# A fused attention and feed-forward layer on one core: the projection of batches 1 to 3 moved, in one-bank pieces, between the attention turns of the batch before

## What is computed

```
x = x + _layernorm(attention(_layernorm(x)))     # x: 4 batches, 1024 tokens, 256 channels, f32
  q, k, v = binlinear(x, W, b)                   # W replaced by mean|W| of its row times sign(W)
  16 heads of 16: softmax(q k^T * 0.25) v, then binlinear(y, Wp, bp)
x = x + _layernorm(ffn(_layernorm(x)))
  h = silu(tlin(x, w1)) * tlin(x, w2)            # 256 -> 1024, ternary weights, a scale for each row
  h = gelu(tlin(h, h1)); h = gelu(tlin(h, h2))   # 1024 -> 1024
  tlin(h, w3)                                    # 1024 -> 256
```

## Time and profile before

| | |
|---|---|
| median of 3 runs | 1319.59 us (1319.3 to 1322.22) |
| the profiled execution | 1320.33 us, its span 1318.6 us |
| PE busy | 1195.9 us (91%) |
| ACT busy | 770.9 us (58%) |
| DVE busy | 558.4 us (42%) |
| POOL busy | 35.0 us (3%) |

### The profile page before, as it was taken

The page is one execution under the profiler, slowest core; times in us unless marked ns, Lnnn a source line. Parts: engine busy times, 40 slices in busy tenths (PEclk is TensorE's granted clock), DMA queues, the critical chain, the costliest instruction groups (busy, mean ns, idle before and its releaser), DMA issues.

```text
span 1318.6 us, 19216 instructions
## 1 busy us (share of the span) xinstructions
PE 1195.9 (91%) x6696; PEld 734.9 (56%) x6696; DVE 558.4 (42%) x1013; ACT 770.9 (58%) x920; POOL 35.0 (3%) x30
## 2 busy tenths in 40 slices
PE   4965999999999999964999999989999999999997
PEld 3741222222222222212788888878888878888886
DVE  7941112111111112043664766727657457475633
ACT  4955999999999999964423324224342243332421
POOL 5220000000000000000000000000000000000000
PEclk9986999999999999977999999989999989999999
DMA  5998576667777776712000101001001001010000
GB/s 159 351 274 209 111 150 129 117 117 141 129 129 129 134 153 120 156 46 64 1 33 0 45 20 34 33 2 33 32 1 64 1 30 36 1 32 1 13 4 16
DMA packets 49946, 107.19 MB, mean 81 GB/s; under 512 B 5856, under 2 KB 22624, under 8 KB 49880
## 3 DMA queue, kind: packets, MB, share of 16 engines
q1 hardware_dynamic: 49880, 106.31, 34.8%
HBM read 71.91 MB, written 45.88 MB: 89 GB/s over the span
## 4 chain that ended last, share of the span: by engine, by line
PE 51%; DVE 1%; issue 1%; ACT 0%; DVEq 0%; ACTq 0%
PE ffn_ps L1136 23%; PE ffn_ps L1137 23%; PE ffn_ps L1164 2%; PE ffn_ps L1165 2%; PE side_ps L1120 1%; PE side_ps L1129 1%; DVE ln_stats L1273 0%; DVE zn L1284 0%; DVE zn L1325 0%; DVE x L1308 0%; DVE zn L1298 0%; DVE x_lo L1315 0%; DVE zn L1301 0%; DVE zn L1335 0%; DVE ln_mean_var L1277 0%
## 5 line engine op out<-in xcount | busy, mean ns | idle before, releaser
L912 ACT ACTIVATE probs<-s_ps 128x1024 f32<-128x1024 f32 x512 | 471.5, 1131 | 25.8 <-PE s_ps L863 25.7
L1137 PE MATMUL ffn_ps<-h_lo,W 128*128 128x512 f32 x1024 | 401.1, 392 | 0.0
L1136 PE MATMUL ffn_ps<-h_hi,W 128*128 128x512 f32 x1024 | 401.1, 392 | 0.0
L872 PE MATMUL y_ps<-probs,v_st 128*17 128x512 f32 x2048 | 273.1, 605 | 37.2 <-DVE y_sb L949 10.0
L1227 ACT ACTIVATE hid<-ffn_ps,scales 128x512 f32<-128x512 f32 x128 | 81.0, 685 | 232.6 <-PE ffn_ps L1137 227.7
L1136 PEld LDWEIGHTS ffn_ps<-h_hi,W 128*128 128x128 f32 x1024 | 192.4, 188 | 42.0
L1137 PEld LDWEIGHTS ffn_ps<-h_lo,W 128*128 128x128 f32 x1024 | 192.4, 188 | 42.0
L863 PEld LDWEIGHTS s_ps<-q_st,k_st 50*128 50x128 f32 x1024 | 78.7, 187 | 240.1 <-ACT probs L912 228.0
L863 PE MATMUL s_ps<-q_st,k_st 50*128 50x512 f32 x1024 | 194.4, 453 | 14.9 <-DVE y_ps L934 9.4
L941 DVE TENSOR_SCALAR low_bits<-W 128x1408 int32 (+1 forms) x16 | 14.3, 894 | 289.5 <-DMA W<-w_scr 289.5
L1349 DVE CAST h_hi<-hid 128x512 fp32r<-128x512 f32 x128 | 53.4, 417 | 183.7 <-ACT hid L1227 183.1
(11 more groups left out here) (103 smaller groups left out, 943.2 us busy)
## 6 DMA issues: line engine op xcount, KB each, us to landing
q_st<-q_scr SPq DMA_DIRECT2D x96, 128.0 KB, 6.7
k_st<-k_scr SPq DMA_DIRECT2D x96, 128.0 KB, 7.0
w_scr<-ffn_w SPq DMA_DIRECT2D x16, 704.0 KB, 12.7
W<-w_scr SPq DMA_DIRECT2D x16, 704.0 KB, 11.6
q_scr<-part SPq DMA_DIRECT2D x16, 512.0 KB, 5.7
k_scr<-part SPq DMA_DIRECT2D x16, 512.0 KB, 6.7
y_scr<-y_sb SPq DMA_DIRECT2D x16, 512.0 KB, 3.3
v_scr<-v_aug SPq DMA_DIRECT2D x8, 544.0 KB, 5.4
```

What stands on the lines that cost most here:

```text
L872: i = pe.matmul(y_ps[32 * j:32 * j + VCOLS, tb * BLK:(tb + 1) * BLK], v_st[u][:, s, VCOLS * j:VCOLS * (j + 1)], probs[m % 2][j // 2][:, j ...
L912: act.activation(probs[m % 2][pp][:, :, :], s_ps[a % 3][:, :, :], ACT.Exp, scale=SCALE).then_inc(probs_ready, 1)
L1136: pe.matmul(bank_of(t)[:, :], w, hi[:, k, :].bitcast(form), start=(k == 0), stop=False)
L1137: mm = pe.matmul(bank_of(t)[:, :], w, lo[:, k, :].bitcast(form), start=False, stop=last)
```

## The change

`project` now makes batch 0 alone, two blocks, written out, and loads the first quad behind its stores. The bound and the flag exist for each batch. The three later batches are projected inside `attention`, which is written out over all 256 turns, 64 for each batch (`TURNS_OF_BATCH`). A batch is projected in the 64 turns of the batch before it, in two windows of 28 turns, one for each block of 512 tokens; the constants `AT_...` say in which turn of a window a piece stands. `y_ps` shrinks to one bank, which makes room for one bank `p_ps`, through which all pieces pass one after another: PE writes it, DVE reads it (`split_x`, `split_qk`, `scale_v`, `top_norm`), and only then may the next piece write it. ScalarE has no part in the pieces: squares, the root and the power -0.5 move to POOL, copies to DVE. At the start of each batch PE, DVE and SP read the batch's flag into a register and branch over the row maxima (`most_of_rows`), which are now written out for four quads. In the last batch's turns the first block of the tail is prepared in the same way (`prepared`), and the tail starts with its branch. The copy of `y_ps` stands at every eighth turn (`copy_y`), and a quad's first `pv` of a half waits for it.

```diff
+QUADS_OF_BATCH = HEADS // QUAD
+BATCH_BLOCKS = SEQ // BLK
+HALVES = QUADS * BATCH_BLOCKS
+TURNS_OF_BATCH = QUADS_OF_BATCH * BATCH_BLOCKS * ST
+WINDOW = 28
+AT_NORM, AT_TURN, AT_QK, AT_V, AT_SUM, AT_TOP, AT_SPREAD = 2, (3, 4), (6, 9, 12, 15), (17, 19), 21, 23, 25
...
-            with sp.Fori(0, BATCH - 2) as b:
-                body(b, True)
-            body(BATCH - 2, False, (range(0, 2), range(2, 3)))
-            body(BATCH - 1, False)
-            for u in range(2):
-                sp.wait_ge(quads.m_loaded[u], 16 * 2)
+                sp.wait_ge(stored[u], 16 * (STORES + 1))
+            load_quad(sp, q_scr, k_scr, v_scr, quads, 0, 0)
+            store_shift()
+            sp.wait_ge(zeros_stored, 16)
+            sp.wait_ge(quads.m_loaded[0], 16 * 2)
...
+        y_ps = ctx.enter_context(nc.psum_tensor("y_ps", [P, BLK], F32))
+        p_ps = ctx.enter_context(nc.psum_tensor("p_ps", [P, BLK], F32))
...
+            def projected(b, t):
+                u, r = window(t)
+                n = BATCH_BLOCKS * (b - 1) + u
+                for m in range(QK):
+                    if r == AT_QK[m] + 1:
+                        store_part(b, u, n, m)
+                if r == AT_TURN[1] + 1 and n + 1 < PROJECTED:
+                    load_xb(n + 1)
+                if r == AT_V[1] + 4:
+                    store_v(b, u, n)
+                if u == BATCH_BLOCKS - 1:
+                    if r == AT_V[1] + 2:
+                        load_first_quad(b)
+                    if r == AT_V[1] + 5:
+                        sp.wait_ge(v_stored, 16 * BATCH_BLOCKS * b)
+                        load_v(sp, v_scr, quads, b * QUADS_OF_BATCH, 0)
+                    if r == AT_SPREAD + 2:
+                        store_shift(b)
+                        sp.wait_ge(shift_stored, 16 * (b + 1))
+                        load_shift(b * QUADS_OF_BATCH, m_loaded[0])
...
+            def ln_rstd(n):
+                pool.wait_ge(var_done, TILES * (n + 1))
+                pool.tensor_tensor(std[:, :], mean_var[:, :, 1], eps_row[:, :], ALU.add).then_inc(std_done, 1)
+                pool.wait_ge(std_done, n + 1)
+                pool.tensor_tensor(rstd[:, :], std[:, :], power[:, :], ALU.pow).then_inc(rstd_done, 1)
...
+                pool.tensor_tensor(square[:, m, :], qk[m % 2][:, :], qk[m % 2][:, :], ALU.mult)\
+                    .then_inc(square_done, 1)
...
+            def pv(turn):
+                n, s = divmod(turn, ST)
+                g = n // BATCH_BLOCKS
+                pe.wait_ge(probs_ready, PAIRS * (turn + 1))
+                if s == 0 and n:
+                    pe.wait_ge(y_copied, n)
...
+            def turn_x(b, u, n, c):
+                pe.wait_ge(norm_done, TILES * (n + 1))
+                if c:
+                    pe.wait_ge(x_read, CT * n + 1)
+                elif u:
+                    pe.wait_ge(norms_read, n)
+                elif b > 1:
+                    pe.wait_ge(column_done, 2 * (b - 1))
+                for t in range(TILES):
...
+            def project_qk(n, m):
+                pe.wait_ge(x_read, CT * (n + 1))
+                if m:
+                    pe.wait_ge(qk_read, QK * n + m)
+                for c in range(CT):
+                    w = signs[:, m // CT, c, (m % CT) * P:(m % CT + 1) * P]
+                    pe.matmul(p_ps[:, :], w, x_hi[:, c, :], start=(c == 0), stop=False)
+                    i = pe.matmul(p_ps[:, :], w, x_lo[:, c, :], start=False, stop=(c == CT - 1))
+                i.then_inc(qk_done, 1)
...
+            def projected(b, t):
+                u, r = window(t)
+                n = BATCH_BLOCKS * (b - 1) + u
+                for c in range(CT):
+                    if r == AT_TURN[c]:
+                        turn_x(b, u, n, c)
+                    if r == AT_V[c]:
+                        project_v(n, c)
+                for m in range(QK):
+                    if r == AT_QK[m]:
+                        project_qk(n, m)
+                if r == AT_SUM:
+                    sum_squares(n)
+                if u == BATCH_BLOCKS - 1:
+                    if r == AT_TOP:
+                        turn_top(b)
+                    if r == AT_SPREAD:
+                        spread_bound(b)
...
+                if t in (20, 22):
+                    project_y((t - 20) // 2)
+                if t in (36, 38):
+                    turn_x1((t - 36) // 2)
+                if t == 46:
+                    turn_bits()
...
+            for b in range(BATCH):
+                if b:
+                    pe.wait_ge(flag_set, b)
+                wide = pe.value_load(const.wide_range[:, b:b + 1], min_val=0, max_val=1)
+                with pe.If(wide):
+                    most_of_rows(b)
+                if b == 0:
+                    pe.wait_ge(y_cleared, 1)
+                for t in range(TURNS_OF_BATCH):
+                    turn = b * TURNS_OF_BATCH + t
+                    scores(turn)
+                    if turn:
+                        pv(turn - 1)
+                    if b + 1 < BATCH:
+                        projected(b + 1, t)
+                    else:
+                        prepared(t)
+            pv(TURNS - 1)
...
+            def copy_y(n):
+                dve.wait_ge(pv_done, ST * (n + 1))
+                if n >= 2:
+                    dve.wait_ge(y_stored[n % 2], 16 * (n // 2))
+                dve.tensor_copy(y_sb[n % 2][:, :], y_ps[:, :]).then_inc(y_copied, 1)
...
+            def split_qk(n, m):
+                slot, k = m % 2, QK * n + m + 1
+                dve.wait_ge(qk_done, k)
+                if k > 2:
+                    dve.wait_ge(square_done, k - 2)
+                dve.tensor_scalar(qk[slot][:, :], p_ps[:, :], const.alpha[:, m:m + 1], const.bias[:, m:m + 1],
+                                  ALU.mult, ALU.add).then_inc(qk_read, 1)
+                dve.wait_ge(qk_read, k)
+                if k > 2:
+                    dve.wait_ge(part_stored[slot], 16 * 2 * ((k - 1) // 2))
+                dve.tensor_copy(part_hi[:, slot, :].bitcast(F32R), qk[slot][:, :]).then_inc(hi_done, 1)
+                dve.wait_ge(hi_done, k)
+                dve.tensor_tensor(part_lo[:, slot, :], qk[slot][:, :], part_hi[:, slot, :], ALU.subtract)\
...
+                if t in (6, 8, 10, 12):
+                    invert_sums(dve, tail_in, 0, (t - 6) // 2)
+                if t == 14:
+                    divide_y(dve, tail_in, 0)
...
+                    if turn % 13 == 11 and turn // 13 < QUADS:
+                        check_w(2 * (turn // 13))
+                        check_w(2 * (turn // 13) + 1)
...
-            pe.wait_ge(bits_done, 1)
-            pe.transpose(bits_ps, top_row_bits[:, :], ident[:, :]).then_inc(bits_turned, 1)
-            project_y(0)
-            turn_x1(0)
-            pe.wait_ge(bits_done, 3)
-            inexact = pe.value_load(any_low[:, :], min_val=0, max_val=1)
+            inexact = pe.value_load(tail_in.any_low[:, :], min_val=0, max_val=1)
...
-            residual(0, 0, 0)
-            low_of_x1(0)
```

801 lines of the change are left out of this document (538 added, 263 removed).

## The result

The changed kernel takes 1340.67 us (median of 4 runs, 1338.24 to 1341.49) against 1319.44 for the kernel before (4 runs, 1316.71 to 1322.22). The ratio is 1.0158 with a 95% interval of [1.0133, 1.0183]: 1.6% slower, where 1293 us and a gain were forecast. The profiled execution took 1338.24 us, its span 1336.5.

A forecast was written before the change was run, and what follows sets the result against it. ACT was taken to bound attention and PE the feed-forward part. From 1320.3 us, -50.9 (earlier start), +38.3 (ACT's idle time) and -15 (tail) gave 1292.7, written as 1293, range 1283 to 1303.

The forecast's parts named there:

- Attention starts sooner: Start of attention: first exponential at about 63.5 us instead of 114.42, -50.9 us, with bounds of 60 and 67.
- The gap at the end: Last batch: `sums` takes 20 us to land, so the copy of `y_ps` is 4 us late, bounds 0 and 12.
- The prediction's own sign of being wrong: Profile after: forecast wrong if PE's waits inside attention name DVE or POOL behind a piece, or feed-forward exceeds 691 us.
- At each later batch's start: Three batch starts in attention: PE's flag load (1.26 us) and branch (0.37) lose 1 us each, 3 in all.
- the branches miss: Rival, batch starts: branches over 256 matmuls cost the far price, 5.6 us more each; 1313 us, chance 0.15.
- The pieces: Projection pieces in attention's turns: each less 0.2 us of slack, 6.8 us a block, 40.8 for six.
- the pieces cost their full length: Rival, projection pieces in attention: no slack, 9.1 us a block, +14, 1307 us; chance 0.09.
- The rival of hidden pieces: Rival, attention: PE's 0.3 us slack in each turn hides most, 5 us a block, 1282 us; chance 0.14.
- `y_ps` in one bank: Attention: copy hides in 0.78 us, except where DVE splits the fourth tile; 2 us in three batches.
- DVE or POOL hold PE up: Rival, attention: late DVE or POOL work on the pieces' one bank stops ACT; at 0.8 us a piece 1336; chance 0.05.
- The tail: Attention's end to feed-forward: first matmul at 610.6 instead of 627.53, -16.9, less 2 for half clock: -15 us.

The follow-up runs named there:

- e13: e9 with the row maxima as a loop over quads, so that each branch passes over 64 matmuls instead of 256; 1291.87 us, ratio 0.9799 to the kernel before.
- e3: Changed kernel with the x block loaded ahead of the second quad, `y` and `sums` loaded earlier, weight chunks checked 13 turns later; 1310.51 us.
- e2: Changed kernel with the row maxima of one quad instead of four behind each flag (64 matmuls, not 256); 1330.52 us in one run.
- e6: Changed kernel with half of each q, k and v piece left out (no matmuls on the low halves of x); 1331.76 us in one run.
- e9: e3 with PE's piece moved from ahead of its turn's scores to behind them, ahead of `pv`; 1299.88 us, ratio 0.9849 to the kernel before.
- e4: Changed kernel with POOL's squares waiting until DVE's subtraction is done; 1341.17 us in one run.
- e12: Kernel before with only the loop of the feed-forward part written out; 1304.59 us, ratio 0.9883.
- e15: Changed kernel with the flag tile `any_low` moved out from ahead of the hidden tiles, which begin 32 bytes earlier; 1330.51 us, ratio 1.0085 to before.
- e18: Kernel before with a 4-byte tile ahead of the hidden tiles, which then begin 32 bytes later; 1331.07 us in one run.

## Why the prediction was wrong

The sum gave 1292.7 us, the profiled execution took 1338.2. The 45.5 us between them, by the prediction's own steps:

**Attention starts sooner: right in kind, 5.8 us too good** (-45.1 instead of -50.9). 4.6 of it is PE's first branch, 4.98 us instead of 0.37; e13, where that branch is short, begins 5.1 us sooner.

**The gap at the end: failed.** "I take 20 us" for the way of `sums` and 4 us for the copy, with 12 as the bound; the wait was longer and cost 15. Two stops of the same kind, at turn 3 of batch 0 and turn 41 of batch 2, were no term at all: 17 us. The prediction looked for what is queued behind a wait only where the kernel before had a gap. The change put DVE's copy of `y_ps` and PE's transposes between turns into the path of every exponential, so each wait on a DMA ahead of them on DVE, PE or in SP's queue had to be listed. Together 28 us too low; e3, which gives these landings time, took the three stops away and shows it. The prediction's own sign of being wrong came out here: PE waits inside attention name DVE, 8.1 us of them behind the transposes of x and 22.8 behind the copy of `y_ps`.

**At each later batch's start: failed.** 3 us were taken, 15.4 came. The step that failed is the price of the branch, 0.37 us taken from one over 64 matmuls where 3.3 to 4.0 came; the flag's load, taken at 1.26, took only 0.30 to 0.49. The rival "the branches miss" got a chance of 0.15 and described what happened, at 17 us on top of the 3 where 12 came, and 3 more at the first where 5 came. Its condition, that 256 matmuls passed over cost the far price, is shown by e2, where 64 cost 0.2 to 0.35 us in the same place.

The Trainium skill, "Runtime: NRT & Kernel Launch", section "Instruction fetch mechanics", says that a taken branch stalls where its target isn't in the current window of two pages, and gives blocks of 256 instructions and room for 2048 on TensorE. An estimate from these: 256 matmuls with their weight loads are at least 512 instructions, which leaves two such blocks and not the 2048. The forward branches agree with the two blocks. The back-branches don't settle it: the one over two quads in the kernel before (L895, 384 matmuls) took 0.21 to 0.22 us in each of its six taken passages, and the one of the feed-forward part (816 matmuls) was cheap in 11 of 28 passages and dear in 17.

The rival's 1313 and the 28 us of the landings make 1341, but by luck: the pieces cost 7 us more than in that sum, the branches some 3 less and the tail 8 less.

**The pieces: mis-sized by 7 us.** 48 us instead of 40.8, as the 0.2 us of slack taken off each was the latency of a start (e6). The rival "the pieces cost their full length" has the mechanism right, and the measured 8.0 us a block lies midway between the forecast's 6.8 and its 9.1, whose way back of 0.2 us was 0.1. By the prediction's own terms its bounds are about 5.0 and 9.5 us a block, not 5.7 and 9.1. The rival of hidden pieces is refuted for this order, and e9 shows where PE's slack lies.

**`y_ps` in one bank**: 2 us predicted at turn 17, 2.9 came, for another reason in part (POOL beside DVE, e4). **DVE or POOL hold PE up**: not by their work, but this rival named the right chain, a bank behind which the scores stand; what was late were the transfers ahead of it.

**The tail: 8 us better than forecast**, -23.3 instead of -15, but by two terms that the prediction didn't have, so that part of its number is chance. The gap fell by 17.9, as forecast (16.9). The two dear back-branches of the kernel before, 15.5 us, were cheap in this profile, and the placement of the hidden tiles cost 10 (e12, e15, e18). Neither has to do with what the change is for.

5.8 + 28 + 12 + 7 + 1 - 8 = 46. Of these the landings and the batch starts are the mechanisms that the prediction had wrong, 40 us.

## What to carry to other kernels

When work is put into a full engine's chain, list for each queue in that chain everything that stands ahead of the critical instruction and waits on a transfer; each such wait becomes a stop, however idle the engines look. Read slack from the engine's sum over a turn and from the side that is waited for, never from the distance between a signal and the start behind it. And when a load is moved ahead of its use, look at what it now stands in front of. Put a branch over as little code as will do, and compare the start addresses of the tiles that a long row of matmuls reads before and after an edit.
